# A graph layer over 100,000 rows: bfloat16 centring, a segment sum on VectorE, index copies moved from GpSimd to VectorE

## The reference

```python
deg = maximum(segment_sum(ones, dst, N), 1.0); norm = deg ** -0.5
h = maximum(layernorm(x), 0)                       # over the 128 features, no affine part
msg = (h[src] @ W1 + (h[src] * h[dst]) @ W2) * (norm[src] * norm[dst])
hN = segment_sum(msg, dst, N) + h @ W1
y = where(hN >= 0, hN, 0.2 * hN)
out = x + y / maximum(sqrt(sum(y * y, axis=1)), 1e-12)
```

## Time and profile before

| | us |
|---|---|
| median of 3 runs | 1258.09 |
| lowest, highest | 1256.14, 1296.67 |
| span of the profiled execution, first to last instruction | 904.7 |
| median less span | 353.4 |

### The profile page before, as it was taken

The page is one execution under the profiler, slowest core; times in us unless marked ns, Lnnn a source line. Parts: engine busy times, 40 slices in busy tenths (PEclk is TensorE's granted clock), DMA queues, the critical chain, the costliest instruction groups (busy, mean ns, idle before and its releaser), DMA issues.

```text
span 904.7 us, 21801 instructions
## 1 busy us (share of the span) xinstructions
PE 724.0 (80%) x6300; PEld 701.2 (78%) x6300; DVE 800.7 (89%) x2616; ACT 780.3 (86%) x3211; POOL 692.5 (77%) x694
## 2 busy tenths in 40 slices
PE   1399989888898897798798889878979887978930
PEld 1398878888887887798798788878978887878830
DVE  6778999999999989897898899788989888989991
ACT  0389999999999897899899899897998899979960
POOL 1777878878888878888888788788878878877643
PEclk9999999999999998999899999898998999989975
DMA  2912757566574675476466656645755665665532
GB/s 68 314 51 75 260 173 236 195 212 235 187 260 166 198 249 172 163 230 219 172 197 218 201 187 231 204 166 176 239 206 170 212 241 166 211 215 178 184 124 84
DMA packets 68938, 172.92 MB, mean 191 GB/s; under 512 B 14411, under 2 KB 34542, under 8 KB 62674
## 3 DMA queue, kind: packets, MB, share of 16 engines
q1 hardware_dynamic: 50002, 135.41, 44.3%
q0 software_dynamic: 18816, 36.08, 12.8%
HBM read 96.89 MB, written 77.04 MB: 192 GB/s over the span
## 4 chain that ended last, share of the span: by engine, by line
POOL 70%; issue 19%; DVE 4%; ACT 2%; DMA 1%; POOLq 1%; PE 1%; SPq 0%; DVEq 0%; ACTq 0%
POOL xd L487 23%; POOL xs L487 23%; POOL out L492 22%; POOL stage L498 2%; POOL sstage L503 1%; DVE xo L866 1%; DMA out<-oe,sstage 1%; ACT junk L1082 0%; DMA out<-xo 0%; ACT ybuf L1143 0%; DVE oe L855 0%; DVE bst L818 0%; DVE agg L910 0%; DVE ybuf L874 0%; SPq L334 0%
## 5 line engine op out<-in xcount | busy, mean ns | idle before, releaser
L1223 PE MATMUL pt<-ident,xin 128*128 128x128 f32 x784 | 233.5, 298 | 97.5 <-DVE bst L818 97.5
L1226 PE MATMUL pt<-nident,bst 128*128 128x128 f32 x1568 | 303.2, 296 | 0.0
L492 POOL DMA_INDIRECT out<-oe,sstage x196 | 244.9, 1250 | 53.9 <-issue 52.6
L1226 PEld LDWEIGHTS pt<-nident,bst 128*128 128x128 f32 x1568 | 268.0, 214 | 0.0
L487 POOL DMA_INDIRECT xs<-in_x,stage x196 | 213.9, 1091 | 53.3 <-issue 53.3
L487 POOL DMA_INDIRECT xd<-in_x,stage x196 | 206.0, 1051 | 59.8 <-issue 59.8
L1082 ACT ACTIVATE junk<-ybuf 128x128 bf16<-128x128 f32 x772 | 248.6, 474 | 0.0
L1236 PE MATMUL pu<-w,ct 128*128 128x128 f32 x1568 | 206.9, 280 | 17.8 <-ACT ct L1066 17.7
L1236 PEld LDWEIGHTS pu<-w,ct 128*128 128x128 f32 x1568 | 188.8, 193 | 22.5 <-ACT ct L1066 22.5
L1223 PEld LDWEIGHTS pt<-ident,xin 128*128 128x128 f32 x784 | 121.4, 155 | 108.3 <-issue 63.0
L1082 ACT ACTIVATION_READ_ACCUMULATOR junk<-ybuf 128x1 f32 x772 | 202.6, 335 | 0.0
(11 more groups left out here) (146 smaller groups left out, 1280.4 us busy)
## 6 DMA issues: line engine op xcount, KB each, us to landing
xin<-in_x SPq DMA_DIRECT2D x96, 512.0 KB, 4.1
out<-xo SPq DMA_DIRECT2D x48, 1024.0 KB
srow<-src_rows SPq DMA_DIRECT2D x49, 256.0 KB, 6.3
edge_rows<-oe SPq DMA_DIRECT2D x49, 256.0 KB
same<-same_segment SPq DMA_DIRECT2D x49, 128.0 KB
xs<-in_x,stage POOLq DMA_INDIRECT x196
xd<-in_x,stage POOLq DMA_INDIRECT x196, 2.6
out<-oe,sstage POOLq DMA_INDIRECT x196
```

Of the source, the lines that this page charges most:

```text
L492: pool.indirect_dma_start(out=out, out_offset=bass.IndirectOffsetOnAxis(ap=index, axis=0), in_=rows, in_offset=None, bounds_check=row_limi ...
L1223: pe.matmul(pt[:, q % 2, f], xin[:, s.buf(), col * D:(col + 1) * D], ident[:], is_transpose=True, start=True, stop=False)
L1226: last = pe.matmul(pt[:, q % 2, f], mean[:, s.buf(0, 2), col:col + 1].to_broadcast([P, D]), nident[:], start=False, stop=True)
```

## The change

- The mean is subtracted in bfloat16 parts. VectorE splits the mean: the upper half of its float32 word is read as a bfloat16, the rest is subtracted out, twice (`mean_part`, two operations of 16 columns). TensorE turns the 48 columns of parts of all 16 rows with one bfloat16 product against the negative identity `nidb`, ScalarE evacuates it to `turned_mean`, and every piece then adds one bfloat16 product of `pick` (which selects a row's three parts) and `turned_mean` in place of the float32 product. `turn_quarter(0)` waits for that evacuation.
- The segment sum `esum = agg + pe_d` is made by VectorE, so that TensorE needs two products per column of edges and ScalarE's `hdt` copy goes. `prod` reads `pe_d` from PSUM.
- VectorE copies the indices of a step for gathers and scatter at once (`stage_rows`), seven steps ahead; GpSimd's two copies go, and it increments two semaphores that nobody waits for.
- One `count_one` stands between the wide addition (L1033) and the wide rectifier (L1038), `degrees` behind the rectifier, `norms_of` at the start of the next step behind the scan; three output rows stand together.
- Before the loop: list loads are split over SP's and ScalarE's queues and the weights loaded behind them; source and destination list are turned and copied to `idx` before the segments' ends are computed; GpSimd clears `idx` first.

```diff
@@ vector
+            def mean_part(s, d, part):
+                h = s.buf(d, 2)
+                words, tops = mean_words(h), mean_tops(h).rearrange("p (t w) -> p w t", w=3)
+                if part == 0:
+                    dve.tensor_tensor(words[:, 0, :], words[:, 1, :], tops[:, 1, :], ALU.subtract).then_inc(part_done, 1)
+                else:
+                    dve.wait_ge(part_done, s(d + 1))
+                    dve.tensor_tensor(words[:, 2, :], words[:, 0, :], tops[:, 0, :], ALU.subtract).then_inc(parts_done, 1)
...
+            def stage_rows(s):
+                dve.tensor_copy(stage[:, s.buf(STAGED, XBUFS), :],
+                                idx[:, bass.ds(s(STAGED), 1), :, :, :].rearrange("p o a q h -> p (o a q h)")
+                                ).then_inc(staged, 1)
...
+                if has(i, 1) and has(i, -1):
+                    norms_of(s, 1)
                 if has(i, -1):
                     dve.wait_ge(u_evac, s() * NQ)
                     leaky_quarter(s, 0)
                     dve.wait_ge(scan_done, s())
-                    dve.wait_ge(hdt_done, s())
-                    dve.tensor_tensor(prod[:, h, :], agg[:, h, :], hdt[:, h, :], ALU.mult).then_inc(prod_done, 1)
+                    dve.tensor_tensor(esum[:, h, :], agg[:, h, :], pe_d[:], ALU.add)
+                    dve.tensor_tensor(prod[:, h, :], agg[:, h, :], pe_d[:], ALU.mult).then_inc(prod_done, 1)
...
+                        mean_part(s, 1, 0)
                     if has(i, -2):
                         out_dense(s, 8, 9)
+                    if has(i, 1):
+                        mean_part(s, 1, 1)
                     if has(i, 2):
                         count_one(s, 2, 1, 0)
                     if has(i, -2):
-                        out_dense(s, 9, 10)
-                    if has(i, 2):
-                        count_one(s, 2, 1, 1)
-                    if has(i, -2):
-                        out_dense(s, 10, 11)
-                    if has(i, 2):
-                        degrees(s, 2)
-                    if has(i, -2):
-                        out_dense(s, 11, 12)
-                    if has(i, 2):
-                        norms_of(s, 2)
+                        out_dense(s, 9, 12)
...
+                    if has(i, 2):
+                        count_one(s, 2, 1, 1)
@@ scalar
-                if has(i, -1):
-                    act.wait_ge(et_done, s())
...
-                    act.copy(hdt[:, s.buf(-1, 2), :], pe_d[:]).then_inc(hdt_done, 1)
                 if has(i, 0):
+                    act.wait_ge(mean_turned, s(1))
+                    act.copy(turned_mean[:], pt[0:3 * TD, 1, 0:P]).then_inc(mean_evac, 1)
                     relu_quarter(0)
@@ tensor
-                        last = pe.matmul(pt[:, q % 2, f], mean[:, s.buf(0, 2), col:col + 1].to_broadcast([P, D]),
-                                         nident[:], start=False, stop=True)
+                        last = pe.matmul(pt[:, q % 2, f], pick[0:3 * TD, col:col + 1].to_broadcast([3 * TD, D]),
+                                         turned_mean[:], start=False, stop=True)
...
+                def turn_means():
+                    pe.wait_ge(parts_done, s(1))
+                    pe.matmul(pt[0:3 * TD, 1, 0:P], mean_tops(s.buf(0, 2)), nidb[:], start=True, stop=True
+                              ).then_inc(mean_turned, 1)
+                    pe.wait_ge(mean_evac, s(1))
...
                 if has(i, 0):
-                    pe.wait_ge(bn_done, s(1))
+                    if has(i, -1):
+                        pe.wait_ge(t_evac, s() * NQ)
+                    turn_means()
                     turn_quarter(0)
...
-                        pe.matmul(pe_m[:, f], hdt[:, h, f], w1[:], start=True, stop=False)
-                        pe.matmul(pe_m[:, f], agg[:, h, f], w1[:], start=False, stop=False)
+                        pe.matmul(pe_m[:, f], esum[:, h, f], w1[:], start=True, stop=False)
@@ gpsimd
-                pool.wait_ge(staged, s(d + 1))
-                if has(i, d + 1):
-                    stage_gather(s, d + 1)
+                pool.sem_inc(p_gather)
...
+                if i is None or i >= STAGED - AHEAD:
+                    pool.wait_ge(staged, s(AHEAD - STAGED + 1))
...
-                    pool.wait_ge(sstaged, s(-2))
-                    if has(i, -2):
-                        stage_scatter(s, -2)
+                    pool.sem_inc(p_scatter)
```

More of the change, by code:

```diff
@@ L127, in gnn_preln_kernel @@
         hd = sb("hd", [P, 2, TE, D])
-        hdt = sb("hdt", [P, 2, TE * P])
+        esum = sb("esum", [P, 2, TE * P])
         agg = sb("agg", [P, 2, TE * P])
@@ L410, in _ @@
         def _(pool):
+            pool.memset(idx[:], 0).then_inc(s_blank, 1)
             pool.memset(ident[:], 0.0).then_inc(s_zero, 1)
@@ L611, in _ @@
             dve.wait_ge(s_ident, 1)
-            dve.tensor_scalar(nident[:], ident[:], -1.0, None, ALU.mult).then_inc(s_const, 1)
+            dve.tensor_scalar(nidb[:], ident[:], -1.0, None, ALU.mult)
+            with nc.allow_low_precision(reason="one of three terms is 1, the others 0"):
+                dve.tensor_reduce(pick[:], ident[:, 0:3 * TD].rearrange("p (t w) -> p t w", w=3), AX.X, ALU.add
+                                  ).then_inc(s_const, 1)
             dve.wait_ge(s_nat, 16 * (6 + 3 * len(whole(QF))))
@@ L700, in _, with turned_index @@
                 dve.wait_ge(u_back, 112)
-                local(lambda ins: uchain(ins, GP // CW * each))
-            dve.tensor_copy(endc[:, 3:4], endc[:, 0:1]).then_inc(s_endc, 1)
-            dve.wait_ge(s_turn, 1)
-            for a in range(3):
-                for h in range(2):
-                    last = dve.tensor_copy(idx[:, :, a, :, h],
-                                           turned[a][:, h * P:h * P + Q].rearrange("p (b q) -> p b q", q=2))
-            last.then_inc(s_idx, 1)
+                gather_lists(lambda ins: uchain(ins, GP // CW * each))
+            dve.tensor_copy(endc[:, 3:4], ucol[:]).then_inc(s_gidx, 1)
+            def turned_index(a, row):
+                for h in range(2):
+                    last = dve.tensor_copy(idx[:, row:row + STEPS, a, :, h],
+                                           turned[a][:, h * P:h * P + Q].rearrange("p (b q) -> p b q", q=2))
+                return last
+            segments()
+            dve.wait_ge(s_turn, 1)
+            dve.wait_ge(s_blank, 1)
+            turned_index(0, 0)
+            turned_index(1, 0).then_inc(s_idx, 1)
+            dve.wait_ge(s_idx, 1)
+            dve.tensor_copy(stage[:, 0:STAGED, :],
+                            idx[:, 0:STAGED, :, :, :].rearrange("p o a q h -> p o (a q h)")).then_inc(s_staged, 1)
+            ends()
+            dve.tensor_copy(endc[:, 3:4], endc[:, 0:1]).then_inc(s_endc, 1)
+            dve.wait_ge(s_turn, 2)
+            turned_index(2, LAG).then_inc(s_idx, 1)
             dve.wait_ge(s_ends, 1)
@@ L891, in _ @@
             stats_guard(Step(0, 0), 0)
+            for part in range(2):
+                mean_part(Step(0, 0), 0, part)
             dve.wait_ge(dd_ready, 1)
@@ L1039, in do @@
                                              ).then_inc(ye_done, 1)
+                if has(i, 2):
+                    degrees(s, 2)
             steps(dve, do, STEPS + 1)
@@ L1165, in _, with turn_lists @@
             pe.matmul(pe_x[0:1, 0:Q], ucol[:, 0:1], ident[0:Q, 0:Q], start=True, stop=True).then_inc(s_urow, 1)
-            pe.wait_ge(s_endc, 1)
-            for a, row in enumerate((0, 1, 3, 4)):
+            def turn_lists(a, row):
                 for h in range(2):
                     last = pe.transpose(turned[a][:, h * P:h * P + Q], natf[:, row, h * P:(h + 1) * P], ident[0:Q, 0:Q])
-            last.then_inc(s_turn, 1)
+                return last
+            pe.wait_ge(s_gidx, 1)
+            turn_lists(0, 0)
+            turn_lists(1, 1).then_inc(s_turn, 1)
+            pe.wait_ge(s_endc, 1)
+            turn_lists(2, 3)
+            turn_lists(3, 4).then_inc(s_turn, 1)
             for k, c in enumerate((0, 1, 2, 4)):
```

104 lines of the change are left out of this document (58 added, 46 removed).

## The result

| | time, us | profiled span, us | mean granted clock |
|---|---|---|---|
| before | 1268.9 (1256.1 to 1296.7) | 904.7 in the trace shown above; 1267.8 in a later one | 0.937; 0.822 |
| changed | 1440.7 (1429.5 to 1467.9) | 1466.3 | 0.713 |

A forecast was written before the change was run, and what follows sets the result against it. GpSimd was taken to pace most of the run. 44 steps x (17.0 - 17.10) = -4.4, +2.9 first and last steps, -1.5 preamble: -3 us, from 1258.09 to 1255 us; range 1246 to 1268, 8 in 10 within 1232 to 1284.

The forecast's parts named there:

- One bfloat16 pass replaces these ... so 0.055 for 128 columns ... Tile: 0.17 us.: TensorE's centring: one bfloat16 pass of 0.055 us replaces two float32 passes of 0.22, taking a tile from 0.33 to 0.17.
- ScalarE's hole: Idle time before ScalarE's first turned quarter: 0.15 latency, 0.67 four tiles, 0.2 pipeline; 1.0 us at full clock, 2.0 slow.
- A wait comes with it, and this is the step that decides: ScalarE evacuates the means, then waits for TensorE's first turned quarter; idle 1.0 to 2.0 us, ScalarE's step 16.55 to 17.6.
- Rival (b): ScalarE waits behind a slow-clocked TensorE in every step: step 17.65 us, 0.55 a step more, 1284 us; chance 0.18.
- None of the 353.4 lies inside the trace; I take it as unchanged: Median 1258.09 us exceeds the profiled span of 904.7 by 353.4; this was added unchanged to the forecast span of 901.7.
- GpSimd paces: GpSimd's gathers, scatters and index copies pace most of the run, 70% of the wait chain; 17.5 us a step, falling to 16.5.
- The clock falls, as expected: TensorE's idle stretch grows from 0.9 to some 4 us a step, so its mean granted clock falls below 0.937.
- the forecast's middle between a fast and a slow start of each step: TensorE restarting after its hole: the step is taken as the mean of 16.55 (full clock) and 17.5 (slow), 17.0 us.

The follow-up runs named there:

- experiment 5: Kernel before, each tile's product taking the mean rounded to bfloat16 straight from the statistics, with no hand-off through ScalarE: 1210.5 us, 0.966 of before.
- experiment 7: Changed kernel with each tile's bfloat16 product run over all 128 rows, zeros in rows 48 to 127: 1207.2 us, 0.964 of before.
- experiment 17: Changed kernel with each indirect gather replaced by a plain load of the same size: 1092.0 us, 0.876 of before.
- experiment 6: Changed kernel with ScalarE's evacuation of the turned means moved ahead of the last five squares of the step before: 1379.1 us, 1.109 of before.
- experiment 1: Kernel before run again without an edit: 1269.48 us, with a profiled span of 1267.8 us.
- experiment 14: Kernel before with each indirect gather of node rows replaced by a plain load of the same size: 872.6 us, 0.690 of before.
- experiment 15: Kernel before with its indirect gathers kept but all taking a constant list, rows 0 to 127: 1271.3 us, 1.019 of before.

## Why the prediction was wrong

- **The step that failed: "One bfloat16 pass replaces these ... so 0.055 for 128 columns ... Tile: 0.17 us."** The pass was priced from float16 passes over 128 rows, and the tile as a sum of passes. With 48 rows it measured 0.41 us at full and 0.62 to 0.63 at half clock. The other terms of ScalarE's hole were right: of the 1.99 us ahead of 707.40, 0.13 is the latency behind the evacuation (705.42 to 705.55; forecast 0.15), 1.67 are four tiles (705.55 to 707.22, where the fifth begins; forecast 0.67), 0.18 the rest (forecast 0.2). The 0.17 is right for 128 rows (experiments 5 and 7). With it, the change would have been 3.6% faster; this one term has the sign of the result in it. The Trainium skill (TensorE: Matmul & The Clock Gate, The mechanism, under "What overlaps and what doesn't") says that weight loads overlap matmuls in flight only when their row group differs; the same section also names the background weight buffer as another way. The traces don't bear out the "only": loads ran ahead between matmuls of the same 128 rows (421.36), and did not between 128 and 48 or 64. Whether the other way explains the first, and what stops it in the second, no run here shows.
- **"A wait comes with it, and this is the step that decides": right in place, too small in size.** ScalarE's idle time stands where the forecast put it, ahead of the first rectifier and released by the centring product. It was to be 1.0 to 2.0 us; it is 1.99 in the step shown, at full clock, 2.61 on average over the 49 steps, whatever ended it, and 2.45 in the step of experiment 17. The second rectifier's 0.86 to 1.03 and the copy's 0.7 were left out: the forecast ended its working with the first quarter, but the second is turned behind it at the same slow pace. And a term is missing on TensorE's side: the turned means wait on ScalarE's queue (702.04 to 705.09), of which experiment 6 won back some 40 us. Rival (b) was thus the right mechanism, at 0.55 us a step where 3.5 came.
- **"None of the 353.4 lies inside the trace; I take it as unchanged": true of the trace, wrong of the timed executions.** It is the indirect gathers' effect on what TensorE releases, inside the execution (experiments 1, 14, 15). That the time of before came out of the sum was no evidence for it, since the 353.4 had been put in. The loss without stalls, 219 us, shows that this was not what turned the sign.
- **GpSimd paces: true of that trace, not of the timed executions,** where it is 51% busy. Its parts came as priced (no copies, transfers of 1.01 to 1.06 us) and, like the sum at 0.60, are no loss: with them and the old centring the time is 0.985.
- **The clock falls, as expected** (0.713). By itself a lower clock need not cost: experiment 7 has 0.770 and gains. But where tiles are on the path it lengthens them, from 0.41 to 0.62 us, and with 72% of the transposes at half clock the forecast's middle between a fast and a slow start of each step was too fast. What the clock alone is worth no experiment separates.

## What to carry to other kernels

Between float32 transposes over all 128 rows, the bfloat16 product over 48 or 64 rows wasn't cheaper: it stopped the weights from loading ahead, and zeros in the unused rows made a tile of 0.41 us one of 0.17. Before an operand is handed from TensorE through another engine and back, count the whole of what it takes off TensorE's lead: the queue it waits in over there, and every tile that could be turned ahead before. And compare the span of the trace with the time before reading a pace from it; 28% were missing here.

## What the runs showed of the hardware that was not expected

Twelve indirect transfers a step (eight gathers, four scatters) made TensorE issue one instruction in 1.40 us for stretches, and what it releases reach ScalarE and VectorE up to tens of us late, at a cost of some 410 us (1285.6 against 872.6 on one chip); four plain loads in place of four gathers took nearly all of it away (906 us), and rows 0 to 127 in every gather nothing (1271 us). The stalls fall into the series of these transfers (92% of ScalarE's remote waits of over 2 us, in 64% of the time, in the second trace of before). A transfer as such was not slower in them (1.00 us, 0.30 apart). One execution of before, the first trace, showed none of this with the same twelve transfers; why is open.
